# Edge attention of a graph network: a wait between the two groups of indirect gathers of a turn

## What is computed

```python
x_src = node_attr[src]                                   # gathered rows
k = ((x_src * (edge_sh @ Wang_k.T)) @ Wlin_k) * (relu(edge_attr @ W1k + b1k) @ W2k)
v = ((x_src * (edge_sh @ Wang_v.T)) @ Wlin_v) * (relu(edge_attr @ W1v + b1v) @ W2v)
alpha = einsum("ehq,qk,ehk->eh", q[dst], Wdot, k)
attn = exp(alpha - amax[dst]) / denom[dst]               # per destination
out = segment_sum(attn * v, dst) @ Wout
```

## Time and profile before

| what | value |
|---|---|
| median of three runs | 4299.57 us (4296.43 to 4299.69) |
| profiled execution, span from first to last instruction | 5039.6 us |
| its own time outside of the span | none is shown; the span stands for it |
| median over profiled span | 0.853 |
| first gather of the attention to the first of its last turn | 1960.67 to 4720.36 us |
| mean granted TensorE clock of the span | 0.911 |
| busy: PE, DVE, ACT, POOL | 82%, 60%, 39%, 38% of the span |
| DMA queues q1 and q0, share of 16 engines | 55.7% and 11.1% |

### The profile page before, as it was taken

The page is one execution under the profiler, slowest core; times in us unless marked ns, Lnnn a source line. Parts: engine busy times, 40 slices in busy tenths (PEclk is TensorE's granted clock), DMA queues, the critical chain, the costliest instruction groups (busy, mean ns, idle before and its releaser), DMA issues. The chain is left out here.

```text
span 5039.6 us, 74127 instructions
## 1 busy us (share of the span) xinstructions
PE 4108.6 (82%) x26543; PEld 3350.2 (66%) x26543; DVE 3024.4 (60%) x4129; ACT 1972.1 (39%) x2885; POOL 1919.0 (38%) x2002
## 2 busy tenths in 40 slices
PE   4667999999999984688888888888888888888832
PEld 4656999999999973465665666666666566666622
DVE  8985544544444342566666666666666666666734
ACT  5754666655665531222222223222223222222313
POOL 5640000000000015555555555555555555555352
PEclk9878999999999985799989999999999999999965
DMA  7998999999998533455555665556666655566433
GB/s 169 188 188 263 298 295 297 294 295 297 292 292 267 182 101 94 133 163 163 164 156 152 166 163 161 162 165 166 164 163 164 166 164 157 159 164 164 141 114 47
DMA packets 1012838, 944.08 MB, mean 187 GB/s; under 512 B 705677, under 2 KB 811929, under 8 KB 1012339
## 3 DMA queue, kind: packets, MB, share of 16 engines
q1 hardware_dynamic: 952099, 814.71, 55.7%
q0 software_dynamic: 60368, 124.52, 11.1%
HBM read 648.66 MB, written 289.97 MB: 186 GB/s over the span
## 5 line engine op out<-in xcount | busy, mean ns | idle before, releaser
L2313 POOL DMA_INDIRECT feats_hops<-x_table,src_s x1616 | 1546.9, 957 | 1223.1 <-PE e_turn_ps L2423 771.8
L1286 PE MATMUL acc<-t_wide,scaled 128*128 128x448 f32 x6860 | 1409.0, 366 | 24.2 <-DVE t_wide L1380 24.2
L1286 PEld LDWEIGHTS acc<-t_wide,scaled 128*128 128x128 f32 x6860 | 1284.3, 188 | 129.2 <-DVE scaled L1398 24.6
L1321 ACT CAST t_wide<-t_ring 128x1568 fp32r<-128x1568 uint8 x490 | 737.7, 1506 | 564.9 <-PE acc L1286 543.8
L1380 DVE CAST t_wide<-t_ring 128x1568 fp32r<-128x1568 uint8 x490 | 478.3, 976 | 733.4 <-PE acc L1286 714.9
L2484 ACT COPY e_out_rows<-e_turn_ps 128x512 f32<-128x512 f32 x404 | 222.1, 588 | 1026.5 <-remote 932.5
L1809 POOL MEMSET l_eps<- 128x1 f32 x1 | 0.1, 104 | 1452.9 <-POOLq L1498 1452.9
L2423 PE MATMUL e_turn_ps<-ident,feats_hops 128*128 128x128 f32 x1616 | 250.3, 296 | 355.6 <-ACT e_out_rows L2484 292.4
L2401 PE MATMUL e_ring_ps<-e_wlin_v,e_x_gv 128*128 128x128 f32 x3232 | 432.7, 281 | 96.9 <-issue 85.6
L2401 PEld LDWEIGHTS e_ring_ps<-e_wlin_v,e_x_gv 128*128 128x128 f32 x3232 | 393.0, 194 | 115.9 <-issue 102.2
L2569 DVE TENSOR_TENSOR e_lw<-e_ring_ps,e_w_t 128x1024 f32<-128x1024 f32 x202 | 247.1, 1223 | 366.9 <-remote 249.6
(11 more groups left out here) (272 smaller groups left out, 5096.2 us busy)
## 6 DMA issues: line engine op xcount, KB each, us to landing
t_ring<-adjacency_bytes SPq DMA_DIRECT2D x490, 512.0 KB, 5.8
sums_table<-e_out_rows SPq DMA_DIRECT2D x202, 576.0 KB
q_first<-hop_zeros_q SPq DMA_DIRECT2D x101, 512.0 KB, 5.9
e_sh<-parts_sh SPq DMA_DIRECT2D x404, 128.0 KB
e_ea<-parts_ea SPq DMA_DIRECT2D x404, 128.0 KB
e_q_rows<-q_first SPq DMA_DIRECT2D x404, 128.0 KB
e_same<-same_row SPq DMA_DIRECT2D x404, 128.0 KB
adjacency_bytes<-lists_staged SPq DMA_DIRECT2D x196, 256.0 KB
```

The lines of the kernel that those rows point to most:

```text
L1286: mm = nc.tensor.matmul(acc[c][:, 0:n], U[p][:, b, :], wide[m % WIDE_RING][:, lo:lo + n], start=(b == 0 and p == 0), stop=(b == NB - 1 and ...
L1321: nc.scalar.copy(into, of).then_inc(wide_act, 1)
L2313: nc.gpsimd.indirect_dma_start(x_rows[i % XR][:, g * GT + t, :], None, x1_table, bass.IndirectOffsetOnAxis(ap=src_ix[:, at:at + 1], axis=0 ...
```

## The change

GpSimd issues the four gathers of the first group of turn i, then waits until all four of them have landed, and only then issues the four of the second group. Since a buffer's semaphore has counted 128 for each earlier turn that used the buffer (16 times K), the value waited for is 16 * (K * (i // XR) + GT).

```diff
                 if i >= XR:
                     pool.wait_ge(p_xt, 2 * (i - XR + 1))
                 for g in range(2):
+                    if g == 1:
+                        pool.wait_ge(x_got[i % XR], 16 * (K * (i // XR) + GT))
                     for t in range(GT):
                         at = group(i, g) * GT + t
                         nc.gpsimd.indirect_dma_start(
```

## The result

The changed kernel takes 4884.65 us (median of 4 runs, 4874.54 to 4888.42) against 4299.63 us, a ratio of 1.1356 (95% interval 1.1342 to 1.1371): **585 us slower**. The forecast was 4419 us, in a range of 4290 to 4580. Its direction was right, its size too small by a factor of almost five.

The account below looks back on a forecast made before the run. PE and ScalarE, handing PSUM back and forth, were taken to set the turn. With the wait POOL's 12.40 us replaces 11.71: 0.69 us over 202 turns, 139 us, less 20 head start, gives 4299.57 + 119 = 4419 us; range 4290 to 4580.

Parts of the forecast that it names:

- the head start: Three gather buffers let POOL fall some 20 to 26 us behind, once, before PE feels it; 20 us taken off the loss.
- Step "in the timed runs", 11.71 us a turn: Attention turn in timed runs: profiled 13.73 us times 0.853, every stage shrinking alike; POOL's 12.40 us then adds 0.69 a turn.
- rival B: Timed attention turn already near POOL's floor of 10.33 us; the change costs 2.07 us a turn, 4698 us; chance 0.17.
- The floor of 10.33 us: Shortest possible attention turn at POOL's pace: eight gathers of 1.257 us plus one semaphore wait of 0.27 us.
- the fifth starts 3.60 us after the fourth: Gather step at the new wait: 3.33 us landing plus 0.27 us semaphore, instead of 1.257 us; 2.34 us of stall.
- The first turn's 4.84 us: From the eighth gather's start to the first turn's transposes, with two turns' loads in flight; high bound of the landing step.
- The low bound: Eighth gather lands in at most 2.23 us when q1 is quiet; 2.50 us to the next start, POOL cycle 11.30 us.
- The span stays near 5040 us: In the profiled execution POOL's idle time covers the stall (2.34 of 4.01 us a turn), so its span does not change.
- no such wait is in the list: Transposes waited for a gather only in the first two turns; no such wait listed from 2100 us on.
- Rival A: Wait covered in timed runs too, by a short landing (0.12) or faster POOL pace (0.19): 4300 us; chance 0.31.
- Rival C: Spread gathers delay SP's store less, returning PSUM to ScalarE earlier: 0.3 us a turn at most, 4239 us; chance 0.07.
- Rival D: The wait does nothing because the fourth gather's count is reached early; chance near zero, within that of no change.

Follow-up runs that it names:

- wait before the second gather: Kernel before plus one GpSimd wait a turn, ahead of the second gather, for all eight gathers of the turn before: 4389.44 us.
- change, light loads: Changed kernel with SP's loads of sh, ea and same cut to 16 of 512 columns, q_rows to one tile, from turn 2 on: 4604.67 us.
- change, seven gathers: Changed kernel without the gather of the eighth tile in each turn, wait count adapted: 4662.96 us.
- wait after six: Kernel before plus a wait for six gathers of the same turn ahead of the seventh, two gathers later than the change: 4768.28 us.
- wait before the first gather: Kernel before plus one GpSimd wait a turn, ahead of the first gather, for all eight gathers of the turn before: 4868.05 us.
- wait after two: Kernel before plus a wait for two gathers of the same turn ahead of the third, two gathers earlier than the change: 4879.29 us.
- two waits: Changed kernel plus a second wait, ahead of the first gather, for all gathers of the turn before: 5271.34 us.
- The profile of the timed regime: Kernel before, unchanged, profiled again: span 4298.8 us, timed 4297.93 us.
- the first trace: Original profile of the kernel before, which the forecast read: span 5039.6 us, against a timed median of 4299.57 us.
- the two new profiles: Kernel before, unchanged, profiled twice more: spans 4298.8 and 4299.8 us, timed 4297.93 and 4298.84 us.
- the second profile: First of the two repeat profiles of the unchanged kernel before: span 4298.8 us, timed 4297.93 us.
- the four kernels compared above: Kernel before (profiled again), changed kernel, and the kernels waiting before the first or second gather for the turn before: 4297.93, 4884.65, 4868.05, 4389.44 us.

## Why the prediction was right and wrong

**The mechanism was right.** The forecast said that GpSimd's cycle would become the turn, with 7 steps of 1.257 us and one long one. It is 8.80 + 4.42 = 13.22 us by the mean of the timeline, 13.24 by the page. POOL's idle time there is only the wait for its own gathers and its issue, so it waits for no other engine; they act on its cycle only through the DMA traffic of SP. Taking 10.26 from it and multiplying by 202 gives 602 us; measured are 585. The waits elsewhere follow the same rule over a range of 970 us. The turn in the table is read from each kernel's own profile, so the table shows that the whole loss lies in these turns; that GpSimd's cycle sets them rests on what it waits for and on the forecasts above.

| kernel | POOL's turn, us | 4298.8 + 202 x (turn - 10.26) | measured |
|---|---|---|---|
| wait before the second gather | 10.79 | 4406 | 4389 |
| change, light loads | 11.80 | 4610 | 4605 |
| change, seven gathers | 12.13 | 4677 | 4663 |
| wait after six | 12.67 | 4786 | 4768 |
| wait before the first gather | 13.16 | 4885 | 4868 |
| wait after two | 13.20 | 4893 | 4879 |
| change | 13.24 | 4901 | 4885 |
| two waits | 15.18 | 5293 | 5271 |

The rule is 5 to 22 us high throughout. Nearly all of that is the head start, which the forecast put at 20 us: from the last gather's start to the end of the span are 269.1 us in the kernel before and 254.4 in the changed one, 14.7 us less. The last transposes start 21.2 us after the last gather before, and 6.0 us after it with the change.

**Step "in the timed runs", 11.71 us a turn: wrong, the larger error.** The forecast scaled the turn by 0.853, and so shared the missing 740 us out evenly over the stages. The profile of the timed regime shows that the attention held nearly all of it: a turn took 13.73 us in the first trace and takes 10.26 here, which is 3.47 x 202 = 701 us of the 741 between the two spans. The stage of the hops was the same in both (1153.17 and 1153.15 us busy of 1240). So 11.71 - 10.26 = 1.45 us a turn, 293 us, was left out. The text had this case as rival B, argued from TensorE's dense hops, and gave it 0.17; the weak step was marked as weak, but the range didn't follow from it. B's mechanism, GpSimd at its floor, was not quite it: TensorE sets the turn, and GpSimd, with 8 x 1.257 = 10.06 us of its own, has 0.2 us to spare. The floor of 10.33 us was itself too high, since the measured turn of 10.26 is below it: the 0.27 us for the semaphore are not paid when the buffer is already free.

**Term "the fifth starts 3.60 us after the fourth": undersized.** It is 4.42 us, 0.82 a turn, 166 us. The 0.27 us for the semaphore was right: 0.26 measured, after a DMA as after TensorE. The landing was mis-sized. The forecast ended it with the last packet (3.33 us taken, 3.45 measured), but the gather's semaphore is complete only 0.71 us later, at 4.16 us. The first turn's 4.84 us held such a stretch too (its last packet started at 3.54 us in the packet records), and had been set aside as a high bound. The low bound had the same flaw: 2.23 us to the last packet, while the last recorded increment of that gather's semaphore came at 2.47. 119 + 293 + 166 = 578 us, against 585 measured.

**"The span stays near 5040 us": wrong.** It was 4886.7 us. Recording as such doesn't stretch this kernel: the spans of the two new profiles agree with the timed runs. Why that one execution had turns of 13.7 us (ScalarE's remote waits of 915.4 us, TensorE's clock at 0.93) stays open. Its trace is also poorer: it holds 11039 semaphore increments by DMAs after 1960 us, the second profile 57079. So "no such wait is in the list" was weak evidence about the gathers, and a wait put down to "remote" in it may be one for a DMA; which one isn't shown.

**Rival A** failed in both halves: the landing is not 2.2 us in that place, and GpSimd's pace is the same 1.26 us in every profile. **Rival C**, faster, didn't come true, but its mechanism was not tested: it needed a GpSimd cycle shorter than the turn, and every wait that spread the gathers made the cycle longer than that. **Rival D** was rightly near zero: 202 waits in the page.

## What to carry to other kernels

A wait for one's own transfers in the middle of an issuing engine's stream puts a latency (landing, and 0.26 us to pass the semaphore on) into the engine's cycle, in every turn; buffers cover it only up to the idle time that the engine has in a turn, and that has to be read from a profile whose span agrees with the timed runs. If the two differ by 17%, the first question is which stage holds the difference, and each stage's waits are then no evidence for the timed regime. Price a landing up to the last increment of its semaphore, from a gather that meets the same traffic, and not up to its last packet.

## What was not expected of the hardware

- The semaphore of a 64 KB gather by GpSimd is complete 2.59 us (median) after its start when q1 moves little, and 4.22 us beside q1's loads. Of this 0.35 and 0.71 us (medians) come after the start of the last packet. The waiting instruction starts 0.26 us after the last increment in both.
- A wait that takes an instruction of its own on GpSimd, behind another wait, costs 0.48 us more: 0.74 us from the complete count to the next gather.
- A wait moved within the turn changes how the gathers and loads meet, so the landing has to be priced anew: the eighth gather's last packet starts between 2.21 and 3.50 us (medians) after its start in the four kernels compared above.
- TensorE's granted clock in the attention was 1.00 before and 0.91 in the changed kernel, where TensorE waited for gathers (PE busy 1526.08 instead of 1786.62 of 1800 us), and 0.87 with two waits; that cost nothing here, since GpSimd set the turn.
